# Causal attention: softmax probabilities turned on TensorE, or a second score pass keys by queries

## What is computed

```python
qkv = jnp.einsum('bnh,hm->bnm', x, w_qkv)
q, k, v = jnp.split(qkv, 3, axis=-1)          # 16 heads of 32
q = rmsnorm(q, q_gamma); k = rmsnorm(k, k_gamma)
q = q * cos + rotate_half(q) * sin
k = k * cos + rotate_half(k) * sin
scores = jnp.einsum('bhqd,bhkd->bhqk', q, k) / np.sqrt(HD)
scores = jnp.where(mask[None, None, :, :], scores, NEG)   # causal
attn = jax.nn.softmax(scores, axis=-1)
out = jnp.einsum('bhqk,bhkd->bhqd', attn, v)
return jnp.einsum('bnh,hm->bnm', out.transpose(0, 2, 1, 3).reshape(b, n, H), w_out)
```

## Time and profile before

| | us |
|---|---|
| median of 3 runs | 2027.5 (2026.59 to 2027.5) |
| the profiled execution | 2008.1 |
| its span, first to last instruction | 2006.2 |
| TensorE busy in the span | 1675.8 |
| VectorE, ScalarE, GpSimd busy | 1241.0, 927.1, 865.4 |

### The profile page before, as it was taken

The page is one execution under the profiler, slowest core; times in us unless marked ns, Lnnn a source line. Parts: engine busy times, 40 slices in busy tenths (PEclk is TensorE's granted clock), DMA queues, the critical chain, the costliest instruction groups (busy, mean ns, idle before and its releaser), DMA issues.

```text
span 2006.2 us, 40434 instructions
## 1 busy us (share of the span) xinstructions
PE 1675.8 (84%) x14233; PEld 1366.2 (68%) x14233; DVE 1241.0 (62%) x2293; ACT 927.1 (46%) x2363; POOL 865.4 (43%) x940
## 2 busy tenths in 40 slices
PE   1648999989994889988789898888889988798987
PEld 1336767647873777777677787777777767687775
DVE  6975656557973455656655566565655655566566
ACT  0002423323321455646556465555655656465565
POOL 1012111105654664563656546355564535546450
PEclk9868999999998899999999999999999999899999
DMA  7100120123424000001111001111100111010001
GB/s 251 45 0 21 33 63 31 42 65 120 157 99 168 33 33 2 34 3 67 64 59 38 1 33 43 54 49 48 38 32 3 54 59 53 29 39 1 2 7 44
DMA packets 58065, 101.04 MB, mean 50 GB/s; under 512 B 3496, under 2 KB 32352, under 8 KB 55328
## 3 DMA queue, kind: packets, MB, share of 16 engines
q1 hardware_dynamic: 56320, 90.01, 13.3%
q0 software_dynamic: 1568, 8.69, 1.4%
HBM read 82.95 MB, written 15.73 MB: 49 GB/s over the span
## 4 chain that ended last, share of the span: by engine, by line
PE 59%; DVE 15%; POOL 13%; issue 8%; ACT 2%; DMA 1%; DVEq 0%; POOLq 0%; ACTq 0%; SPq 0%
PE psum L1166 12%; PE psum L1108 8%; PE psum L1134 5%; PE psum L1145 4%; PE psum L1118 3%; PE psum L1089 3%; PE psum L935 3%; DVE pT L1412 3%; PE psum L1001 3%; POOL rot L618 2%; POOL hl L634 2%; POOL roped L622 2%; POOL roped L615 2%; PE psum L1085 2%; PE psum L1024 2%
## 5 line engine op out<-in xcount | busy, mean ns | idle before, releaser
L819 ACT ACTIVATE prob<-psum,nmax 128x896 f32<-128x896 f32 (+7 forms) x512 | 376.1, 739 | 196.3 <-DVE nmax L1399 157.3
L1108 PE MATMUL psum<-consts,prob 128*128 128x128 f32 x2304 | 345.9, 283 | 94.4 <-DVE pT L1412 92.6
L1399 DVE TENSOR_REDUCE nmax<-psum 128x1 f32<-128x640 f32 (+3 forms) x256 | 261.4, 1021 | 226.4 <-PE psum L1090 226.3
L1166 PE MATMUL psum<-w_s,xnT 128*128 128x384 f32 x1536 | 328.6, 366 | 79.9 <-DVE pT L1412 53.2
L1166 PEld LDWEIGHTS psum<-w_s,xnT 128*128 128x128 f32 x1536 | 285.0, 203 | 102.9 <-DVE pT L1412 64.9
L1108 PEld LDWEIGHTS psum<-consts,prob 128*128 128x128 f32 x2304 | 252.9, 144 | 117.7 <-DVE pT L1412 110.1
L805 ACT ACTIVATE pT<-psum 128x384 f32<-128x384 f32 (+3 forms) x320 | 146.7, 458 | 184.4 <-PE psum L1108 180.4
L1412 DVE COPY pT<-psum 128x512 f32<-128x512 f32 (+1 forms) x320 | 214.4, 670 | 21.0 <-PE psum L1108 19.6
L615 POOL TENSOR_TENSOR roped<-raw,cosG 128x512 f32<-128x512 f32 x64 | 81.6, 1275 | 323.5 <-DVE raw L1460 323.5
L1397 DVE TENSOR_REDUCE nmax<-psum 128x2 f32<-128x256 f32 (+3 forms) x128 | 105.3, 823 | 138.9 <-PE psum L1090 138.8
L606 POOL TENSOR_TENSOR rs<-ms,half_neg 128x16 f32<-128x16 f32 x64 | 186.4, 2913 | 5.3
(11 more groups left out here) (160 smaller groups left out, 3089.1 us busy)
## 6 DMA issues: line engine op xcount, KB each, us to landing
w_s<-w_split SPq DMA_DIRECT2D x16, 1536.0 KB, 6.5
xs<-in_L_attn_x SPq DMA_DIRECT2D x32, 256.0 KB, 2.6
y<-in_L_attn_x SPq DMA_DIRECT2D x32, 256.0 KB, 3.4
out_y<-y SPq DMA_DIRECT2D x32, 256.0 KB, 2.1
arena<-in_L_attn_x SPq DMA_DIRECT2D x3, 2048.0 KB, 8.9
w_split<-arena POOLq DMA_DIRECT2D x4, 1536.0 KB, 5.4
arena<-in_L_ffn_wq SPq DMA_DIRECT2D x8, 512.0 KB, 4.6
arena<-in_L_ffn_wo SPq DMA_DIRECT2D x8, 512.0 KB, 3.7
```

What stands on the lines that cost most here:

```text
L819: act.activation(prob[:, i % 3, a * CH:a * CH + w], src, ACT.Exp, bias=nmax[:, i % 4, a:a + 1], scale=-1.0, accum_out=den[:, s % 2, h:h + ...
L1108: last = pe.transpose(psum[:, bank, n * P:(n + 1) * P], prob[:, i % 3, a * CH + j * P:a * CH + (j + 1) * P], ident)
L1166: last = pe.matmul(psum[:, bank, 0:3 * P], xnT[:, a, k, m * P:(m + 1) * P], w_s[u % 2][:, c, k, :], start=(k == 0 and a + c == 0), stop=(k ...
L1399: dve.tensor_reduce(nmax[:, i % 4, 0:1], psum[:, bank:bank + 2, :].rearrange("p a n -> p (a n)")[:, 0:w], AX.X, ALU.min).then_inc(min_made, 1)
```

## The change

The probabilities are no longer turned. Each unit makes two passes over its scores.

The **row pass** (22 pieces: tiles 0 and 1 with all four heads, 2 and 3 with two, the others with one) computes scores queries by keys as before, with the mask. VectorE takes the minimum into `low`, ScalarE the exponentials for their sum alone: it writes them back over the scores in PSUM (`row_exps_of`). For each **half** of a unit (four query tiles, 512 queries) ScalarE takes the logarithm of the row sums (`log_sum`), VectorE subtracts the minimum and splits the result into high and low parts (`log_sums`), TensorE turns them (`turn_lse`), ScalarE copies them to `lse_rows` (`rows_out`), and two DMAs from SP's queue write them as rows 96 and 97 of the query stack (`lse_row`). The key stacks have ones in those rows, filled once (`k_ones`).

The **second pass** (20 pieces) multiplies key stack by query stack, keys by queries, for each key tile j and the half's queries (`col_scores`); its product is score plus log-sum, and exp of its negative (`col_exps`) is the probability, already divided and already with keys on the partitions. The masked upper triangle of the four diagonal blocks of a half is set to zero on GpSimd (`clear`, an affine_select on 128x2x128 or 128x4x128). `value` then works on up to 512 queries at once. The second pass of a unit starts in its slot 21 and ends in slot 44, so that most of it stands beside the next unit's row pass.

Also: q, k and v of the projection are copied out by VectorE instead of ScalarE; the projection weights have one buffer instead of two; the ring of four banks becomes a deal of all eight, with one or two neighbouring banks for an item; `hl` holds four tiles instead of eight; GpSimd's chunk steps are spread over slots of their own; loads and stores of SP are placed by slot.

```diff
-        pT = held("pT", [2, NT, GH, P])
-        nmax = held("nmax", [4, 2])
-        den = held("den", [2, GH])
-        rden = held("rden", [2, GH])
+        pT = held("pT", [3, GH, CH])
+        low = held("low", [2, GH, NT])
+        den = held("den", [2, GH, NT])
+        lse_l = held("lse_l", [2, GH, 4])
+        lse_r = held("lse_r", [2, GH, 4])
+        lse_rows = held("lse_rows", [2, P])
         ss3 = held("ss3", [2, 16])
         ms3 = held("ms3", [16])
...
+        hl = held("hl", [4, 2, GH, 3, AD], f32r)
+        qH = [held(f"q_half{i}", [GH, CH], f32r) for i in range(3)]
+        kH = [held(f"k_half{i}", [GH, CH], f32r) for i in range(4)]
+        lse_s = held("lse_s", [2, 2, 16], f32r)
...
+                wait(sp, w_ps, u * NT)
+                sp.dma_start(w_s.rearrange("p e k c -> p (e k c)").bitcast(f32), split_d[u % 4]).then_inc(w_in, 16)
...
+            def lse_row(n):
+
+                sp.wait_ge(lse_out, n + 1)
+                for e in range(2):
+                    sp.dma_start(qH[n % 3][STK + e:STK + e + 1, :, :].rearrange("p h n -> p (h n)").bitcast(f32),
+                                 lse_rows[16 * e:16 * (e + 1), n % 2, :]).then_inc(rows_in[n % 3], 16)
...
+            def clear(i):
+
+                u, c, j, k, heads = col(i)
+                lo = (j - 4 * c) * P
+                own = pT[:, k % 3, heads[0]:heads[-1] + 1, lo:lo + P]
+                pool.wait_ge(col_exp, i + 1)
+                pool.affine_select(out=own, in_=own, compare_op=ALU.is_ge, fill=0.0, base=0,
+                                   pattern=[[0, len(heads)], [1, P]], channel_multiplier=-1).then_inc(cleared, 1)
...
+            def log_sum(n):
+
+                u, c = divmod(n, 2)
+                act.wait_ge(row_exp, row_exps(u * NR + (5 if c == 0 else NR - 1)))
+                wait(act, lse_a, n - 1)
+                act.activation(lse_l[:, n % 2], den[:, u % 2, :, 4 * c:4 * c + 4], ACT.Ln).then_inc(ln_made, 1)
+            def col_exps(i):
+
+                u, c, j, k, heads = col(i)
+                bank = BANK_OF["col", i]
+                lo = max(0, j - 4 * c) * P
+                w = CH - lo
+                act.wait_ge(col_ps, i + 1)
...
+                    src = psum[:, bank:bank + 2, :].rearrange("p a n -> p (a n)").rearrange("p (h n) -> p h n", h=GH)
+                act.activation(pT[:, k % 3, heads[0]:heads[-1] + 1, lo:CH], src, ACT.Exp, scale=-1.0).then_inc(col_exp, 1)
...
+                    at = a * (w if t < 2 else CH)
+                    act.activation(flat[:, at:at + w], flat[:, at:at + w], ACT.Exp, bias=low[:, u % 2, h, t:t + 1], scale=-1.0,
+                                   accum_out=den[:, u % 2, h, t:t + 1]).then_inc(row_exp, 1)
...
+                    if half >= 3:
+                        act.wait_ge(col_ps, (half - 3) // 2 * NC3 + (6 if (half - 3) % 2 == 0 else NC3))
+                    act.activation(qH[half % 3][0:STK, :, part], src, ACT.Copy).then_inc(q_out, 1)
...
+            def col_scores(i):
+
+                u, c, j, k, heads = col(i)
+                bank = BANK_OF["col", i]
+                freed("col", i)
+                if j == 0:
+                    pe.wait_ge(rows_in[(2 * u + c) % 3], 32 * ((2 * u + c) // 3 + 1))
+                pe.wait_ge(k_out, u * NT + j + 1)
+                lo = max(0, j - 4 * c) * P
+                w = CH - lo
+                for a, h in enumerate(heads):
+                    out = psum[:, bank + a * w // CH, a * w % CH:a * w % CH + w] if len(heads) == 4 else psum[:, bank + a, 0:w]
+                    last = pe.matmul(out, kH[(2 * u + j // 4) % 4][0:STK + 2, h, j % 4 * P:(j % 4 + 1) * P], qH[(2 * u + c) % 3][0:STK + 2, h, lo:CH],
+                                     start=True, stop=True)
+                last.then_inc(col_ps, 1)
...
+                if j >= 4 * c:
+                    pe.wait_ge(cleared, diags(last_col(k)))
+                else:
+                    pe.wait_ge(col_exp, last_col(k) + 1)
...
+                dve.tensor_tensor(lse_r[:, n % 2], lse_l[:, n % 2], low[:, u % 2, :, own], ALU.subtract).then_inc(lse_a, 1)
+                dve.wait_ge(lse_a, n + 1)
+                made = lse_r[:, n % 2].rearrange("p h t -> p (h t)")
+                dve.tensor_copy(lse_s[:, n % 2, 0, :], made).then_inc(lse_hi, 1)
+                dve.wait_ge(lse_hi, n + 1)
+                dve.tensor_tensor(lse_s[:, n % 2, 1, :], made, lse_s[:, n % 2, 0, :].bitcast(f32), ALU.subtract).then_inc(lse_lo, 1)
...
+            def projected_out(n):
+
+                u, m = divmod(n, NT)
+                c = n // 2
+                bank = BANK_OF["w", n]
+                dve.wait_ge(w_ps, n + 1)
+                wait(dve, turned, c - 1)
...
+COLS_LATE = 3
+VALUE_LATE = 2
+LSE_AT = (8, 25)
+STACK_AT = (21, 22, 23, 24, 29, 30, 35, 36)
+PROJECT_AT = (8, 10, 14, 16, 20, 22, 26, 28)
+TURN_X_AT = (5, 7, 11, 13, 17, 19, 23, 25)
+NORM_X_AT = (3, 5, 9, 11, 15, 17, 21, 23)
+LOAD_X_AT = (-2, 0, 6, 8, 12, 14, 18, 20)
+SQUARE_AT, SUM_AT, POW_AT, SCALE_AT, TURN_AT, HIGH_AT, LOW_AT = 11, 12, 12, 14, 14, 15, 16
+OUT_AT = (30, 33, 35, 37, 49, 51, 52, 53)
+
...
+ROW_AT, COL_AT = row_slots(), col_slots()
+VALUE_AT = [COL_AT[LAST[k]] + VALUE_LATE for k in range(NK)]
+FIRST, END = -NS - 6, (U + 2) * NS + 8
...
+def tensor_items(i):
+    out = [("row", n) for n in ROW_IN.get(i, ())]
+    out += [("col", n) for n in COL_IN.get(i, ())]
+    out += [("lse", n) for n in LSE_IN.get(i, ())]
+    out += [(kind, n) for n in STACK_IN.get(i, ()) for kind in ("q", "k")]
+    out += [("value", n) for n in VALUE_IN.get(i, ())]
+    out += [("y", n) for n in OUT_IN.get(i, ())]
+    out += [("x", n) for n in TURN_X_IN.get(i, ())]
+    out += [("w", n) for n in PROJECT_IN.get(i, ())]
+    return out
...
+HELD = {"row": 1.3, "col": 1.1, "lse": 0.8, "q": 0.8, "k": 0.9, "y": 1.4, "x": 1.5, "w": 1.6}
```

More of the change, by code:

```diff
@@ new lines @@
+LAST = [max(n for n in range(NC3) if COLS[n][0] == k) for k in range(NK)]
+DIAG = [STEPS[k][1] >= 4 * STEPS[k][0] for k, _ in COLS]
+ROW_EXPS = [sum(len(heads) for _, heads in ROWS[:n]) for n in range(NR + 1)]
+DIAGS = [sum(DIAG[:n]) for n in range(NC3 + 1)]
+COLS_LATE = 3
[6 more added lines that the diff above has]
+LOAD_X_AT = (-2, 0, 6, 8, 12, 14, 18, 20)
@@ new lines, with spread @@
+VALUE_AT = [COL_AT[LAST[k]] + VALUE_LATE for k in range(NK)]
+FIRST, END = -NS - 6, (U + 2) * NS + 8
+def spread(table, units, every=1, ahead=0):
+    out = {}
+    for u in range(0, units, every):
+        for n, at in enumerate(table):
+            out.setdefault((u - ahead) * NS + at, []).append(u // every * len(table) + n)
+    return out
+ROW_IN = spread(ROW_AT, U)
+COL_IN = spread(COL_AT, U)
+LSE_IN = spread(LSE_AT, U)
+STACK_IN = spread(STACK_AT, U, ahead=1)
+VALUE_IN = spread(VALUE_AT, U)
@@ L1598, in deal_banks @@
         for n, (kind, idx) in enumerate(items):
-            k = min(range(4), key=lambda m: free[m])
-            bank_of[kind, idx] = 4 + k
-            before[kind, idx] = holder[k]
-            holder[k] = (kind, idx)
-            free[k] = i + n / max(4, len(items)) + HELD[kind]
+            held = HELD.get(kind)
+            if kind == "value":
+                u, c, j = step(idx)
+                if j:
+                    continue
+                kind, idx = "o", 2 * u + c
+                held = VALUE_AT[3 if c == 0 else 11] - VALUE_AT[0 if c == 0 else 4] + 1.6
```

640 lines of the change are left out of this document (314 added, 326 removed).

## The result

| us | before | changed |
|---|---|---|
| median (runs) | 2027.5 (2026.59 to 2028.1) | 2061.06 (2055.55 to 2061.69) |
| span of the profiled execution | 2006.2 | 2060.0 |

The change makes the kernel slower by 1.6%: ratio 1.016, 95% interval [1.0142, 1.0178]. The forecast was 1872, its range ended at 1990.

A forecast was written before the change was run, and what follows sets the result against it. The prediction took TensorE to set the pace. Start 664, unit 0 56, fourteen units 1036, turns of x 15, last unit 52 and tail 27 gave a span of 1850, or 1872 us as median; range 1750 to 1990.

The forecast's parts named there:

- What bounds the kernel now: Kernel before: TensorE sets the pace, losing 9 us a unit, mostly while VectorE has yet to copy turned probabilities.
- TensorE, 62.1 us a unit: TensorE's work in an ordinary unit: net 9.6 us less, from 71.7, as transposes go and second-pass scores come.
- a lower clock: Sign of a wrong forecast: TensorE's granted clock well below 0.96 to 0.98, from more and longer gaps.
- ScalarE, 57.5: ScalarE's work in a unit: copies go, second-pass exponentials add 17.0 us and table loads 5.1.
- ScalarE lump: ScalarE in slots 21 to 1: near 18 us of work where TensorE has 12; 3 us added to the path.
- GpSimd and the clears: Clears of diagonal blocks on GpSimd, priced like products at 0.71 and 1.28 us: 10.8 us a unit more, 53.8 in all.
- slow rival: Clears on GpSimd cost as much as the power: 92 us a unit, 2128 us in all; chance 0.07.
- Where the path runs, 74 us: A unit's path: 38.5 us for slots 16 to 29, 3 for ScalarE, 32.5 for slots 5 to 16.
- the rope chain: Slots 16 to 23, projection to stacks: 14.3 us plus 4.7 of clears queued on GpSimd, 19 us for 6.4 slots.
- slots in lockstep: Rival: each slot waits for its busiest engine; maxima 80 us, taken as 82 a unit, 1990 us; chance 0.22.
- The start and the tail: Both ends of the attention stage: first row minimum at 664 us, unit 0 56, last unit 52, tail 27.
- The chances: Odds for the whole change: faster 0.90, same 0.02, slower 0.08.

The follow-up runs named there:

- the fastest version: Changed kernel with one table set loaded once, TensorE making the second pass's scores first, and no row minimum: 1755.0 us, ratio 0.8693.
- experiment 2: Changed kernel with GpSimd's clears of the diagonal blocks and their waits left out: 2044.61 us, ratio 1.012.

## Why the prediction was wrong

**What bounds the kernel now.** Half right. VectorE's copies were waited for, but the row minimum cost 76 us too, partly by holding those copies back; I had read VectorE as covered because it was 62% busy.

**TensorE, 62.1 us a unit.** The count of products and their durations were right: the fastest version has a unit with 62.00 us at a clock of 1.00. It held for the full clock alone. In the changed kernel the mean of fourteen is 72.1, where the clock is 0.90; the fastest version has 63.6 at 0.99, which at 0.90 would be an estimated 70, so the clock is most of it. I had listed a lower clock as a sign that I was wrong and had given it no place in the sum. With the turns of x my sum gave TensorE 63 us of 75, so of the 11 us a unit that the forecast missed (86.0 for 75), 9 are TensorE's busy time; its idle time is 13.9 us where my 75 implied 12. That was the contradiction in it: I let TensorE idle for 12 us a unit and kept durations read at a clock of 0.96 to 0.98.

**ScalarE, 57.5.** Right in size (55 to 57). The table loads were 1.28 and four a unit, as priced, but "ScalarE lump" let them stand in one place as 3 us above the chain; they cost their full length (1.2 to 1.3 us each with the minimum in), 1.5 without the minimum and 2.3 once the rest was fast. The drain of 1380 ns that the Trainium skill adds ("ScalarE: Activation LUTs", What ACT_TABLE_LOAD costs) does not show: 0.01 us lies between each load and the instruction behind it in ScalarE's timeline of the changed kernel,

```profile
1065.04 1.28 ACT L832 ACT_TABLE_LOAD   x1
1066.33 0.22 ACT L832 ACTIVATE lse_l<-den 128x16 f32<-128x16 f32 x1
1066.57 1.28 ACT L848 ACT_TABLE_LOAD   x1
1067.86 0.81 ACT L848 ACTIVATE pT<-psum 128x768 f32<-128x768 f32 x1
```

and leaving out loads of 5.1 us a unit gave back 4.8.

**GpSimd and the clears.** 5.9 us a unit, not 10.8: the price taken from products of two inputs was the wrong row, the cast's 0.41 was the near one. The slow rival, clears at the price of the power, is excluded, and with it the 2.6 us for 256 elements that was an estimate from the Trainium skill ("GPSIMD Engine Reference", Performance versus the Vector engine): 0.417 us measured.

**Where the path runs, 74 us.** This is the step that failed. It took two tight places and let everything else overlap; measured were 86.0. At the first place, the rope chain, TensorE waited 4.0 us in 1100, and experiment 2 finds 0.7 us a unit where 4.7 us of clears were said to stand in the chain. The second, ScalarE's lump with its loads, was put at 3 us; the loads alone cost 4.8. And the sum had no term for the banks' hand-overs and none for the clock: TensorE, VectorE and ScalarE hand the same eight banks round, and in each slot TensorE made first what ScalarE wanted second. With one table set and that order turned (and the deal with it) the unit is 76.8 and the kernel 1912.2, inside the range. The slots in lockstep (0.22) came nearest with 82 and its 1990; the slot maxima, 80, lack 6 us, and I take the latency within a slot and the clock, which they leave out, for the rest. That lockstep is no law of the slots is shown by the 67.1 us of the fastest version with the same table of slots: without the loads' 5.1 us the maxima would still be 75.

**The start and the tail.** 667.4 for 664 and 60.9 for 56 were near. The last unit, to its last row minimum at 2008.2, took 75 us and not 52, and the tail 52 and not 27. Windows of the tail in the changed kernel, and TensorE's last group:

```profile
1990.00:2010.00 20.00, 16.89 (x80) 9.26 (x80) 9.30 (x10) 13.93 (x23) 3.72 (x8) 0.74 0.00 1
2010.00:2030.00 20.00, 17.28 (x75) 6.95 (x77) 4.61 (x10) 11.29 (x15) 2.08 (x4) 0.74 0.04 14
```

```profile
2045.00 5.16 PE L1194 MATMUL psum<-w_out,oT 128*128 128x512 f32 x8 [0.91 <-DVE oT L1484]
```

In the last unit TensorE has no projections, and its clock is 0.74 just where I had it fast. The kernel before has none there either and kept 0.95, with 737 matmuls in 73.3 us where now 461 stand in 127.3. The last output products stand alone behind everything, 5 us. Before, the last unit to the end was 73.3 us, so the second pass's lag of a unit costs 54 us here, as much as the whole slowdown, and unit 0, 60.9 us where it was 80.4, gives back 20. Even the fastest version needs 94 us from its sixteenth unit to the end.

**The sum of the misses** against the forecast's span of 1850: start 3, unit 0 5, fourteen units 153, last unit and tail 48, together the 210 us measured.

**The chances.** 0.08 for slower stood on one dear instruction. What came was several cheap waits with a clock behind them; a rival of that kind wasn't among mine.

## What to carry to other kernels

When work is taken off the engine that looks like the bound, ask whether it will now wait: here 39% fewer matmuls kept TensorE busy for as long, at a clock of 0.89 instead of 0.94 over the span. Write each engine's order inside a slot so that what the next engine takes first is made first, and look at which banks that order deals (67 to 157 us together). Price a reduction between a product and its consumer even where its engine is half idle (52 to 157 us). Here each of 32 Ln among Exps loaded two tables: load a set that holds both, once. And price the end of a schedule whose second half lags by a unit.
